# A graph attention layer on one core: the first load in two column halves, ScalarE's loads issued singly, and SyncE's branch ahead of its last wait

## What is computed

```python
s_i = x @ attn[:128]
s_j = x @ attn[128:]
e = leaky_relu(s_i + s_j.T, negative_slope=0.2)
e = e + where(adj > 0, 0.0, -1e9)
alpha = softmax(e, axis=1)
out = layernorm(x + alpha @ x)
```

## Time and profile before

| | us |
|---|---|
| median of 3 runs (263.14 to 263.3) | 263.21 |
| the profiled execution | 262.65 |
| its span, first to last instruction | 260.8 |
| PE busy | 247.6 |
| DVE busy | 236.0 |
| ACT busy | 165.8 |

### The profile page before, as it was taken

How to read it: one execution, slowest core, us unless ns; L and a number is a source line. 1 busy time by engine, 2 the same in 40 slices (tenths; PEclk the granted TensorE clock), 3 DMA queues, 4 the chain that set the end, 5 groups by cost and what they waited for, 6 DMA issues and landing times.

```text
span 260.8 us, 5350 instructions
## 1 busy us (share of the span) xinstructions
PE 247.6 (95%) x2117; PEld 240.9 (92%) x2117; DVE 236.0 (90%) x385; ACT 165.8 (64%) x241; POOL 36.7 (14%) x74
## 2 busy tenths in 40 slices
PE   7968899999999999999999999999999999999970
PEld 6646899999999999999999999999999999999970
DVE  1949999999999999999999999999999999999261
ACT  1349989986875798539971797359832995054010
POOL 1000000000330033003300330015000330033022
PEclk9999999999999999999999999999999999999996
DMA  6999999999999999999999999999999930001001
GB/s 198 319 348 348 349 349 347 350 349 348 349 349 359 350 349 356 355 349 348 347 362 349 336 284 363 341 343 285 364 342 343 265 110 0 3 0 44 0 0 43
DMA packets 70236, 71.67 MB, mean 275 GB/s; under 512 B 2881, under 2 KB 68674, under 8 KB 70210
## 3 DMA queue, kind: packets, MB, share of 16 engines
q10 hardware_dynamic: 34592, 34.67, 42.9%
q1 hardware_dynamic: 34594, 34.67, 42.8%
q0 software_dynamic: 1024, 1.97, 2.3%
HBM read 69.21 MB, written 2.10 MB: 273 GB/s over the span
## 4 chain that ended last, share of the span: by engine, by line
PE 90%; DVE 3%; ACT 2%; ACTq 1%; POOL 1%; issue 1%; POOLq 0%; DVEq 0%
PE psum L801 86%; DVE weights L669 1%; ACTq L249 1%; PE psum L754 1%; PE psum L780 1%; PE psum L769 1%; DVE mask_bytes L578 1%; ACT adj_in L345 1%; POOL out_dram L257 1%; DVE mask_t L573 1%; ACT adj_in L352 0%; ACT x_raw L456 0%; PE psum L757 0%; PE psum L759 0%; DVE x_raw L614 0%
## 5 line engine op out<-in xcount | busy, mean ns | idle before, releaser
L801 PEld LDWEIGHTS psum<-xj,weights 128*128 128x128 f32 x2048 | 229.0, 192 | 2.8 <-issue 2.8
L801 PE MATMUL psum<-xj,weights 128*128 128x129 f32 x2048 | 229.3, 275 | 1.8 <-issue 0.9
L669 DVE SCALAR_TENSOR_TENSOR weights<-q_row,r_j,mask_t 128x512 f32<-128x512 f32 x256 | 172.7, 739 | 1.8
L385 ACT ACTIVATE mask_bytes<-adj_in 128x4096 uint8<-128x4096 int32 x27 | 96.9, 3607 | 15.4 <-DMA adj_in<-in_adj_dram 15.4
L560 DVE STREAM_TRANSPOSE mask_t<-mask_bytes 128x1024 uint32<-128x1024 uint32 x27 | 33.4, 1235 | 0.0
L391 ACT ACTIVATE x_raw<-x_raw 128x128 f32<-128x128 f32 x28 | 8.3, 298 | 36.1 <-DVE x_raw L614 35.8
L309 POOL TENSOR_SCALAR neg_mean<-total 128x4 f32<-128x4 f32 x7 | 3.7, 525 | 170.2 <-ACT x_raw L391 170.2
L318 POOL DMA_DIRECT2D out_dram<-x_raw x28 | 14.6, 527 | 20.5 <-ACT x_raw L405 20.4
L379 ACT ACTIVATE mask_bytes<-adj_in 128x2048 uint8<-128x2048 int32 x8 | 15.1, 1897 | 0.0
L398 ACT ACTIVATE unused<-x_raw,neg_mean 128x128 f32<-128x128 f32 x28 | 10.9, 390 | 4.6 <-POOL neg_mean L309 4.6
L405 ACT ACTIVATE x_raw<-x_raw,offset,rstd 128x128 f32<-128x128 f32 x28 | 11.5, 480 | 2.3 <-POOL offset L315 2.3
(11 more groups left out here) (58 smaller groups left out, 59.6 us busy)
## 6 DMA issues: line engine op xcount, KB each, us to landing
adj_in<-in_adj_dram ACTq DMA_DIRECT2D x64, 512.0 KB, 14.7
adj_in<-in_adj_dram SPq DMA_DIRECT2D x64, 512.0 KB, 13.9
out_dram<-x_raw POOLq DMA_DIRECT2D x28, 64.0 KB, 5.3
x_raw<-in_x_dram ACTq DMA_DIRECT2D x4, 128.0 KB, 3.1
x_raw<-in_x_dram SPq DMA_DIRECT2D x4, 128.0 KB, 3.7
x_raw<-in_x_dram ACTq DMA_DIRECT2D x2, 256.0 KB, 6.1
x_raw<-in_x_dram SPq DMA_DIRECT2D x2, 256.0 KB, 6.7
out_dram<-x_raw POOLq DMA_DIRECT2D x4, 32.0 KB, 1.9
```

Source lines behind the costliest of these rows:

```text
L385: nc.scalar.activation(mask_bytes[:, g % BYTE_SLOTS, :, :, :], adj_in[:, g % ADJ_SLOTS, :, :, :], ACT.Sign).then_inc(bytes_ready, 1)
L669: nc.vector.scalar_tensor_tensor(weights[:, slot_of(n, c), :], q_row[:, n * BANK:(n + 1) * BANK], r_j[:, c:c + 1], mask_t[:, (n * PIECES + ...
L801: return nc.tensor.matmul(banks[(n * K + t) % 8][:, 0:D1], weights[:, slot_of(n, c), t * P:(t + 1) * P], xj[:, c, 0:D1], start=(c == 0), s ...
```

## The change

- Piece 0 is loaded in two halves of its columns (`load_first`): eight transfers of 256 KB with runs of 512 B. The first half has a semaphore of its own.
- DVE turns that first half to bytes between its first maximum and its second, and transposes it after the second. It no longer waits for the whole piece before the first weights.
- ACT's transfers: the second half of piece 0 behind copies 0 and 1 of xT, quadrant 2 of piece 1 behind copy 3, quadrant 3 of piece 1 behind the row sums, both of piece 2 behind copy 7, those of piece 3 around `scale_xj(1, PC)`; from then on quadrant 3 of piece g + 2 and quadrant 2 of piece g + 3 behind the conversion of piece g.
- ACT sums all eight chunks of stripe 2, which DVE had shared.
- PE: turns 0 to 3, s_i pieces 0 and 1, turns 4 and 5, s_i 2, turns 6 and 7, s_i 3, the spreading of the maximum, s_i pieces 4 to 7.
- SP: the wait for the last stores stands behind the branch on `again` (and also inside it).

```diff
-    S_J_BY_ACT = slice(2 * SC, 2 * SC + K)
+    S_J_BY_ACT = 2
+        first_half_loaded = sem("first_half_loaded")
+        def load_first(queue, quadrants, f):
+            part = slice(f * P, (f + 1) * P)
+            for q in quadrants:
+                queue.dma_start(adj_in[B * q:B * (q + 1), 0, :, :, part],
+                                adj_v[0, 0, q, :, :, :, part]).then_inc(adj_loaded[0] if f else first_half_loaded, 16)
...
-            for g in range(ALL_PIECES):
+            for f in range(PF):
+                load_first(sp, LOW_HALF, f)
+            for g in range(1, ALL_PIECES):
                 load_piece(sp, LOW_HALF, g)
...
-            sp.wait_ge(last_stored, 16 * Q * (len(FINAL_GROUPS) - EARLY))
             sp.wait_ge(again_ready, 1)
             with sp.If(sp.value_load(again[0:1, 0:1], min_val=0, max_val=1) > 0):
...
+            sp.wait_ge(last_stored, 16 * Q * (len(FINAL_GROUPS) - EARLY))
...
-            load_piece(act, HIGH_HALF, 0)
+            load_first(act, HIGH_HALF, 0)
             for m in range(RB):
                 act.wait_ge(xT_in_psum, m + 1)
                 nc.scalar.copy(...)
-                if m < 4:
-                    load_piece(act, HIGH_HALF[m % 2:m % 2 + 1], 1 + m // 2)
-                if m == K:
-                    act.wait_ge(products_ready, 3)
-                    for c in range(S_J_BY_ACT.start, S_J_BY_ACT.stop):
+                if m < 2:
+                    load_first(act, HIGH_HALF[m:m + 1], 1)
+                if m == 3:
+                    load_piece(act, HIGH_HALF[0:1], 1)
+                if m == 4:
+                    act.wait_ge(products_ready, S_J_BY_ACT + 1)
+                    for c in range(S_J_BY_ACT * SC, (S_J_BY_ACT + 1) * SC):
                         last = nc.scalar.activation(prod[:, c, :], prod[:, c, :], ACT.Identity, accum_out=s_j[:, c:c + 1])
                     last.then_inc(s_j_by_act_ready, 1)
+                    load_piece(act, HIGH_HALF[1:2], 1)
+            load_piece(act, HIGH_HALF, 2)
             act.wait_ge(below_max_ready, 1)
...
             q_piece(0)
-            load_piece(act, HIGH_HALF[0:1], 3)
             act.wait_ge(factors_ready, 1)
             scale_xj(0, 1)
             q_piece(1)
-            load_piece(act, HIGH_HALF[1:2], 3)
             q_piece(2)
             q_piece(3)
+            load_piece(act, HIGH_HALF[0:1], 3)
             scale_xj(1, PC)
+            load_piece(act, HIGH_HALF[1:2], 3)
...
                     half_to_bytes(g, 0)
-                    load_piece(act, HIGH_HALF, g + IN_FLIGHT)
+                    if g > BY_DVE:
+                        load_piece(act, HIGH_HALF[1:2], g + 2)
                     if g < PIECES:
                         scale_xj(g * PC, g * PC + K)
                     half_to_bytes(g, 1)
+                    load_piece(act, HIGH_HALF[0:1], g + 3)
...
                     to_bytes(g)
-                    if g + IN_FLIGHT < ALL_PIECES:
-                        load_piece(act, HIGH_HALF, g + IN_FLIGHT)
+                    if g + 2 < ALL_PIECES:
+                        load_piece(act, HIGH_HALF[1:2], g + 2)
+                    if g + 3 < ALL_PIECES:
+                        load_piece(act, HIGH_HALF[0:1], g + 3)
...
-            sum_products(3, stripe(3))
-            sum_products(2, slice(S_J_BY_ACT.stop, 3 * SC))
+            sum_products(3)
...
             nc.vector.reduce_max(smax[:, 0:1], s_j[:], X).then_inc(row_max_ready, 1)
+            dve.wait_ge(first_half_loaded, 16 * Q)
+            first_part_to_bytes(0)
             dve.wait_ge(max_spread, 1)
...
-            dve.wait_ge(adj_loaded[0], 16 * Q)
-            first_part(0)
+            dve.wait_ge(half_bytes_ready, 1)
+            turn_half(0, 0)
...
                         if g == 0:
-                            first_part(1)
+                            dve.wait_ge(adj_loaded[0], 16 * Q)
+                            first_part_to_bytes(1)
+                            dve.wait_ge(first_bytes_ready, 1)
+                            turn_half(0, 1)
...
-            turn_x(0)
-            for m in range(1, 4):
+            for m in range(4):
                 turn_x(m)
-                s_i_piece(m - 1)
+            s_i_piece(0)
+            s_i_piece(1)
             turn_x(4)
+            turn_x(5)
+            s_i_piece(2)
+            turn_x(6)
+            turn_x(7)
             pe.wait_ge(attn_j_ready, 1)
             s_i_piece(3)
-            for m in range(5, RB):
-                turn_x(m)
-            s_i_piece(4)
             pe.wait_ge(row_max_ready, 1)
...
-            for rb in range(5, RB):
+            for rb in range(4, RB):
                 s_i_piece(rb)
```

More of the change, by code:

```diff
@@ L508, in _, with sum_products @@
         def _(dve):
-            def sum_products(st, c):
+            def sum_products(st):
+                c = slice(st * SC, (st + 1) * SC)
                 dve.wait_ge(products_ready, st + 1)
                 nc.vector.reduce_sum(s_j[:, c], prod[:, c, :], X).then_inc(s_j_ready, 1)
-            def stripe(st):
-                return slice(st * SC, (st + 1) * SC)
             def product_of(st):
@@ L530, in _ @@
             product_of(0)
-            sum_products(0, stripe(0))
+            sum_products(0)
             dve.wait_ge(x_loaded[1], 16 * Q)
             product_of(1)
-            sum_products(1, stripe(1))
+            sum_products(1)
             dve.wait_ge(x_loaded[2], 16 * Q)
@@ L537, in _, with turn_half, first_part_to_bytes @@
             product_of(3)
-            sum_products(3, stripe(3))
-            sum_products(2, slice(S_J_BY_ACT.stop, 3 * SC))
-            dve.wait_ge(s_j_ready, STRIPES)
+            sum_products(3)
+            dve.wait_ge(s_j_ready, STRIPES - 1)
             dve.wait_ge(s_j_by_act_ready, 1)
             nc.vector.reduce_max(smax[:, 0:1], s_j[:], X).then_inc(row_max_ready, 1)
+            def turn_half(g, f):
+                part = slice(f * P, (f + 1) * P)
+                src = mask_bytes[:, g % BYTE_SLOTS, :, :, part].bitcast(u32).rearrange("p k r w -> p (k r) w")
+                dst = mask_t[:, g % MASK_SLOTS, f, :, :].rearrange("p i k -> p (i k)").bitcast(u32)
+                nc.vector.transpose(dst.rearrange("p (r a) -> p r a", a=B), src).then_inc(mask_ready if f else half_mask_ready, 1)
+            def first_part_to_bytes(f):
+                part = slice(f * P, (f + 1) * P)
+                nc.vector.tensor_scalar(mask_bytes[:, 0, :, :, part], adj_in[:, 0, :, :, part], 0.0, None,
+                                        ALU.is_gt).then_inc(first_bytes_ready if f else half_bytes_ready, 1)
+            dve.wait_ge(first_half_loaded, 16 * Q)
+            first_part_to_bytes(0)
             dve.wait_ge(max_spread, 1)
@@ L566, in first_to_bytes @@
                                         ALU.is_gt).then_inc(first_bytes_ready, 1)
[L568 to L578, removed]
-                                                        ALU.is_gt)
-                if f == 0:
-                    bytes_of_part.then_inc(half_bytes_ready, 1)
-                    dve.wait_ge(half_bytes_ready, 1)
-                else:
-                    bytes_of_part.then_inc(first_bytes_ready, 1)
-                    dve.wait_ge(first_bytes_ready, 1)
-                turn_half(0, f)
-            dve.wait_ge(adj_loaded[0], 16 * Q)
-            first_part(0)
+            dve.wait_ge(half_bytes_ready, 1)
+            turn_half(0, 0)
             def group_of(n):
```

## The result

| kernel | runs | median us | range us | ratio to before (95%) |
|---|---|---|---|---|
| before, beside it | 20 | 263.02 | 262.25 to 263.91 | |
| after | 20 | 261.28 | 260.56 to 263.67 | 0.9942 [0.9925, 0.9958] |
| after, once more (e9) | 12 | 261.11 | 260.19 to 263.25 | 0.9941 [0.9920, 0.9962] |

The ratio of e9 is to the kernel before in its own set, 262.77 us.

A forecast was written before the change was run, and what follows sets the result against it. PE's unbroken run of products bounds the kernel, so only its start or what follows it can gain. First weights 2.75 us earlier, 0.6 lost at chunk 6: 262.65 minus 2.15 is 260.5, plus 0.56 for the median: 261.1; range 260.3 to 262.7.

The forecast's parts named there:

- PE's order costs nothing except turn 4: At the start, PE's reordered turns and s_i pieces all lie beside ACT and DVE work, except turn 4.
- ACT's transfers: At the start, moving ACT's issues takes the 2.86 us issue off the path: copy 4 at 12.45, 2.97 us earlier.
- Eight sums: ACT's sums take 2.34 us, giving back 1.17 of 2.97; row maximum at about 15.35 instead of 17.27.
- Issues before the exponentials: Two ACT issues behind the last copies set the first weights: 19.0 instead of 21.76, 2.75 us earlier.
- The price of 512 B runs: Piece 0's load at 27 ns a packet, 24.5 a slot: 6.3 us instead of 5.9, piece 1 landing 0.5 late.
- The point of decision: Price of 512 B packets above which rival (b), a slower kernel, holds: 33 ns a slot, 36 ns a packet.
- Where the gain is stopped: At piece 1's landing before chunk 6: weights 6 end at 26.9, PE's run 2.15 us earlier, 0.6 lost in a hole.
- Later pieces come each 6.0 us against 7.16 of PE, so the lead grows and hides ACT's later issues: After piece 1, pieces arrive faster than PE uses them; PE has no holes after the one before chunk 6.
- SP's wait: At the kernel's end, moving SP's wait behind its branch was taken as 0; a stall there, +0.5 us, chance 0.03.
- Rival (a): Smaller transfers move at 284 GB/s, not 347: piece 1 lands 1.4 late, gain 1.25, 262.0 us; chance 0.20.
- Rival (b): A 512 B packet costs what a 1 KB packet does, 50 ns: weights 6 3.3 late, 266.5 us; chance 0.09.
- (c): No change: piece 1's delay from the packet price eats the earlier start's gain, 263.2 us; chance 0.05.

The follow-up runs named there:

- e9: The kernel after, unchanged, run once more beside e10 and e11 on one chip; 261.11 us, ratio 0.9941 to before.
- e3: The kernel after with SP's wait for the last stores back ahead of its branch; 260.83 us, ratio 0.9912 to before.
- e10: The kernel after with piece 0 loaded whole in 1 KB runs and PE's order as before; 261.28 us, ratio 0.9938 to before.
- e7: The kernel before with only ACT's transfers placed as in after, later ones too, piece 0 whole; 259.94 us, ratio 0.9906 to before.
- e6: The kernel after, halves kept, with DVE's conversion of the first half moved behind the second maximum; 260.95 us, ratio 0.9957 to before.
- e5: The kernel after with ACT's transfers from piece 4 on placed as before; 263.56 us, ratio 1.0032 to before.
- e2: The kernel after with SP's two transfers of piece 1 also cut into column halves of 512 B runs; 267.93 us, ratio 1.0186 to before.
- e11: The kernel after with only SP's quadrants of piece 0 in column halves, ACT's whole in 1 KB runs; 263.92 us, ratio 1.0051 to before.
- e8: The kernel before with only PE's order and ACT's eight sums as in after, all transfers as before; 263.33 us, ratio 1.0026 to before.

## Why the prediction was right

The median, 261.28, lies 0.2 above the forecast, and part of that closeness is luck: the gain was forecast as 2.15 and measured as 1.74, but the sum started from 263.21, the median of three runs, where that of twenty is 263.02.

*PE's order costs nothing except turn 4:* right. Copy 4 was forecast at 12.45 and came at 12.73 (12.42 in e3). But e10 shows that the text gave this part too small a role: it costed the order and never asked what the eight sums would cost without it.

*ACT's transfers:* right, and the heart of it. No issue over 1.6 us stood ahead of 16 us but one of 1.70 at 15.52, behind the sums. e7 shows that this step, with the later placement, gives the gain alone, and more by its median.

*Eight sums:* row maximum forecast at 15.35, measured 15.76 (15.45 in e3); second maximum 16.68, measured 16.99 (16.68 in e3). The early conversion's place was right; that it is worth nothing (e6) was not said, though the forecast's own step, with the gain stopped at piece 1, implied it.

*Issues before the exponentials:* the first weights came at 18.66, 18.35 in e3 and 17.65 in e9, not 19.0. I had queued two issues behind the last copies, ahead of the exponentials; in the rows ACT's queue issues them while its sums and copies still run (in after at 13.93, 14.90 and 15.52), and the exponentials start at 17.59, waiting for DVE. The error is harmless, since the time was not set there.

*The price of 512 B runs:* the term that was mis-sized. Taken 27 ns a packet and 24.5 a slot; measured 34 and 27.9. Piece 0 then takes 256 x 27.9 = 7.1 us, not 6.3, and piece 1 lands not 0.5 late but 0.8 in e9 (23.95 against 23.15) and 1.7 in after; over the six traces with both halves on both queues and piece 1 whole it was 0.3 (e5) to 1.7. The point of decision, 33 ns a slot, was not reached. (The Trainium skill, DMA: Bandwidth & Descriptors, Why small descriptors are slow (HBM only), gives a packet about 3 cycles over its beats of 32 bytes; worked out from that, 19 against 35 here, a ratio of 0.54. The slots measured 27.9 / 45.5 = 0.61, so this estimate would have undersized the price as I did.)

*Where the gain is stopped:* right in its place, piece 1's landing plus 1.91, 0.63 and 0.71. Forecast for the end of weights 6 was 26.9; e3 has 27.05, e9 27.26, after 28.18. The gain there was 2.04, 1.83 and 0.91 against 2.15. The hole before chunk 6 is 2.09 us (1.26 in e3, 2.17 in e9), not 0.6: the start came earlier and the data later than forecast, and only the second of these errors moves the end.

*"Later pieces come each 6.0 us against 7.16 of PE, so the lead grows and hides ACT's later issues":* this sentence failed. Piece 2 was converted 6.3 us after piece 1 in e9, 7.3 in after and 7.5 in e3, so the lead hardly grew or shrank. e5 shows that the old issues are not hidden (2.3 us), and e3 a small hole at chunk 14. It is the new placement, which I had counted at nothing, that keeps PE running. The forecast came out right because the kernel has that placement.

*SP's wait:* right, worth 0 (e3). "The end followed PE's branch" was half of it: POOL's drain of 2.674 us ended with it. PE's branch fell from 3.83 us to 3.32 in after, and POOL was then last. From the end of PE's run to the end of the span it was 9.7 us before and 9.5 in after.

Rival (a), the smaller transfers, gave 262.0 for a piece 1 that lands 1.4 late. Its rate, 284 GB/s, is what the halves moved at (283 in after, 290 in e9); it was nearer there than the forecast's slot of 24.5 ns, which is 334 GB/s. After's own profile has its landing too, and its time of 261.77 is near it; e9 and e3 land earlier. Its reason, the size of a transfer, was not separated from the length of a run: a half is both shorter in its runs and smaller. The equal packet counts of e2 and e11 fit the run's length. (The formula that stands beside rival (a) is given by the Trainium skill, DMA: Bandwidth & Descriptors, Anatomy of one DMA — SWDGE (gpsimd) path, as a fit to transfers of GpSimd's path, while SP and ACT issue here; by the prediction's own terms 4 us more give 264.6, not 264.7.) Rival (b) wanted 50 ns and got 34. Against (c) stands the interval, whose upper end is 0.9958.

## What to carry to other kernels

When an issue blocks its engine, count the packets outstanding and put the issue behind work that nobody waits for, all through the kernel and not only where the stall is seen first: once the start is earlier, the next blocked issue is uncovered. Before splitting a transfer by columns for an early first part, ask when the *next* piece is wanted, because shorter runs delay all that is queued behind them. Two queues that together bring one tile should have packets of one size; otherwise the one with the shorter ones brings fewer bytes in the same time. And a wait of PE can cost more than its own length, since its clock can be low behind it (e6, e8).

## What the runs showed of the hardware

- Two queues on the same 16 engines get equal packets, not equal bytes, while both have work: 1582 to 1584 packets, 1.57 to 0.79 MB in 8 us (e2).
- 512 B packets ran at 283 GB/s (290 in e9) where 1 KB ran at 347. (The Trainium skill, DMA: Bandwidth & Descriptors, Specifications, gives 512 B as the least for line rate. Here it is not enough.)
- A single instruction fetch took 1.15 us of one DMA engine (e3).
- POOL's drain at the barrier took 2674 ns in before, after and all eleven experiments, whatever else changed.
- After PE had waited, the granted clock stood at 0.50 over 32 to 36 us (e2, a wait of 7.18 us), at 0.57 over 29 to 33 (e6, waits of 0.72 and 2.70) and at 0.50 over 20.7 to 22.7 (e8, a wait of 3.76), the level of 1.2 GHz or near it, though PE was busy again. In after, which waited 2.09 us, it stayed at 1.00.
